# Carry scan over chunk ends: seven steps of one product each in place of four steps of up to three

## The reference

```python
# _ln: layer norm over the features
s = sigmoid(silu(x @ s_w1.T + s_b1) @ s_w2.T + s_b2)
u = (x @ B_w.T + B_b) * s                      # [b, t, 128]
def step(h, u_t):
    h = h @ A.T + u_t                          # A is 128 x 128
    return (h, h)
_, hs = scan(step, 0, u over t)
y = hs @ C_w.T + C_b + x @ D_w.T + D_b
attn = y * sigmoid(x @ g_w.T + g_b)            # x = x + ln(attn(ln(x)))
out_shared = sq_relu(xf @ Ws1) @ Ws2           # ffn, x = x + ln(ffn(ln(x)))
```

## Time and profile before

| what | value |
|---|---|
| median of 3 runs | 879.07 us (879.03 to 879.16) |
| the profiled execution, device time | 878.09 us |
| its span | 876.3 us |
| granted TensorE clock, mean over the span | 0.996 |
| DMA, mean | 84 GB/s |
| chain that ended last | ACT zn and DVE adds of the last rows, under 1% of the span each |

### The profile page before, as it was taken

One profiled execution on the slowest core, in us unless ns is written; L12 is line 12 of the kernel. 1 busy time (PEld: TensorE's weight loads), 2 busy tenths in 40 slices (PEclk: granted clock), 3 DMA queues, 4 the chain that ended last, 5 costly groups with the idle time before them and its releaser, 6 DMA issues. The chain is left out here.

```text
span 876.3 us, 12884 instructions
## 1 busy us (share of the span) xinstructions
PE 846.2 (97%) x4120; PEld 699.9 (80%) x4120; DVE 600.0 (68%) x1380; ACT 299.5 (34%) x530; POOL 374.5 (43%) x502
## 2 busy tenths in 40 slices
PE   5999999999999999999999999999999999999985
PEld 3778888888888888888888888888888888888874
DVE  5856775777757778577775777577775767844684
ACT  3431333323432334324342233333343323432333
POOL 0252336254344444253451633616334344435455
PEclk9999999999999999999999999999999999999999
DMA  9320303023220232221232230302323021122112
GB/s 306 127 97 0 97 27 146 21 97 96 95 99 24 73 96 97 98 72 44 77 117 77 96 96 16 144 35 97 96 83 111 3 94 49 49 96 97 49 48 97
DMA packets 17309, 73.23 MB, mean 84 GB/s; under 512 B 2643, under 2 KB 5075, under 8 KB 11094
## 3 DMA queue, kind: packets, MB, share of 16 engines
q1 hardware_dynamic: 17238, 72.38, 23.7%
HBM read 38.82 MB, written 33.55 MB: 83 GB/s over the span
## 5 line engine op out<-in xcount | busy, mean ns | idle before, releaser
L1624 POOL TENSOR_TENSOR xres<-work,xres 128x512 f32<-128x512 f32 x64 | 82.5, 1289 | 62.3 <-DVE work L1196 61.5
L433 PE MATMUL TM<-gw_hi,xT_hi 128*128 128x512 f32 x256 | 104.3, 407 | 0.0
L1588 POOL TENSOR_TENSOR rsz<-rsz,negh 128x1 f32<-128x1 f32 x64 | 39.4, 615 | 149.3 <-DVE rsz L1285 149.3
L433 PE MATMUL TM<-dw_hi,xT_hi 128*128 128x512 f32 x256 | 103.1, 403 | 0.0
L435 PE MATMUL TM<-dw_hi,xT_lo 128*128 128x512 f32 x256 | 100.5, 392 | 0.0
L435 PE MATMUL TM<-gw_hi,xT_lo 128*128 128x512 f32 x256 | 100.5, 392 | 0.0
L434 PE MATMUL TM<-gw_lo,xT_hi 128*128 128x512 f32 x256 | 100.0, 391 | 0.0
L434 PE MATMUL TM<-dw_lo,xT_hi 128*128 128x512 f32 x256 | 99.8, 390 | 0.0
L1588 POOL TENSOR_TENSOR rsv<-rsv,negh 128x1 f32<-128x1 f32 x64 | 35.8, 560 | 122.5 <-DVE rsv L1192 122.5
L1628 POOL TENSOR_TENSOR work<-work,xres 128x512 f32<-128x512 f32 x62 | 79.5, 1293 | 17.5 <-ACT work L908 17.5
L908 ACT ACTIVATE work<-TM,nmz,rsz 128x512 f32<-128x512 f32 x62 | 48.2, 778 | 69.3 <-POOL nmz L1598 69.1
(11 more groups left out here) (146 smaller groups left out, 2071.7 us busy)
## 6 DMA issues: line engine op xcount, KB each, us to landing
xin<-in_x SPq DMA_DIRECT2D x16, 1024.0 KB, 5.6
xres<-in_x SPq DMA_DIRECT2D x16, 1024.0 KB, 5.6
x_scratch<-xres SPq DMA_DIRECT2D x16, 1024.0 KB, 5.3
out<-work SPq DMA_DIRECT2D x30, 512.0 KB, 2.9
xres<-in_g_w_t SPq DMA_DIRECT2D x1, 1024.0 KB, 7.3
xres<-in_D_w_t SPq DMA_DIRECT2D x1, 1024.0 KB, 7.1
work<-in_Ws SPq DMA_DIRECT2D x2, 512.0 KB, 9.5
out<-work SPq DMA_DIRECT2D x4, 256.0 KB, 2.0
```

Source lines behind the costliest of these rows:

```text
L433: eng.matmul(ps, lhs[0], rhs[0], start=first, stop=False)
L1588: return eng.tensor_tensor(dst, src, negh[:, 0:n], ALU.pow)
L1624: eng.tensor_tensor(xres[:, j, :], work[:, j, :], xres[:, j, :], ALU.add).then_inc(S["x1_ok"], 1)
```

## The change

Steps 1 to 4 become steps 1 to 7 of one product each, with s = 1, 2, 4, ... 64: 7 products of 127, 126, 124, 120, 112, 96 and 64 columns in place of 10. The recurrence within the chunks is now steps 8 to 14. The powers A^24, A^96 and A^384 are no longer made, 21 products in the prologue for 24. The order of all engines is written anew, in the tails, the bodies and the prologue: among the rest the statistics and `h2` of DVE's tail stand elsewhere between the adds, `hs_low(3)` stands ahead of `ft_low(1)`, `SG(1)` ahead of `T(6)` and `T(7)`, and `s_gate(1)` of the prologue ahead of the high parts of f1 and f2. DMAs, their sizes and SP's order are the same. Line numbers below 460 stay, those of DVE's part shift by 12 (`scan_add`'s 1169, 1172 and 1175 are 1157, 1160 and 1163).

```diff
--- before.py
+++ after.py
@@ -76,7 +76,7 @@
-        POW = [1, 2, 3, 4, 5, 6, 7, 8, 16, 24, 32, 64, 96, 128, 256, 384, 512]
+        POW = [1, 2, 3, 4, 5, 6, 7, 8, 16, 32, 64, 128, 256, 512]
...
@@ -458,14 +458,11 @@
                     for j in range(L - 1):
                         m = eng.matmul(SC[:, 0:P], apt[:, idx[L - 1 - j], :], u[:, j, :],
                                        start=(j == 0), stop=(j == L - 2))
-                elif i <= 4:
-                    s = 4 ** (i - 1)
-                    reps = [r for r in (1, 2, 3) if r * s < P]
-                    for r in reps:
-                        m = eng.matmul(SC[:, r * s:P], apt[:, idx[L * s * r], :], carry[:, 1:1 + P - r * s],
-                                       start=(r == 1), stop=(r == reps[-1]))
+                elif i <= 7:
+                    s = 2 ** (i - 1)
+                    m = eng.matmul(SC[:, s:P], apt[:, idx[L * s], :], carry[:, 1:1 + P - s], start=True, stop=True)
                 else:
-                    j = i - 5
+                    j = i - 8
                     prev = carry[:, 0:P] if j == 0 else u[:, j - 1, :]
                     m = eng.matmul(SC[:, 0:P], apt[:, 0, :], prev, start=True, stop=True)
@@ -607,33 +604,31 @@
 
             def first_tail(b, rep):
                 a = (b, rep)
-                G(*a, 0, {1: 0})
-                scan_step(*a, 1)
-                G(*a, 1, {0: 2, 1: 3, 2: 4})
-                scan_step(*a, 5)
-                G(*a, 2, {1: 6, 2: 7})
-                scan_step(*a, 8)
-                scan_step(*a, 9)
-                G(*a, 3, {0: 10})
+                G(*a, 0, {0: 0, 2: 1})
+                scan_step(*a, 2)
+                G(*a, 1, {0: 3, 1: 4, 2: 5})
+                scan_step(*a, 6)
+                G(*a, 2, {0: 7, 1: 8, 2: 9})
+                scan_step(*a, 10)
                 scan_step(*a, 11)
+                G(*a, 3, {0: 12, 2: 13})
+                scan_step(*a, 14)
 
             def tail(b, rep):
                 a = (b, rep)
-                G(*a, 0)
-                scan_step(*a, 0)
-                W1f(*a, 1, 0, {0: 1, 2: 2})
-                scan_step(*a, 3)
-                W1f(*a, 1, 1, {2: 4})
-                scan_step(*a, 5)
-                G(*a, 1, {1: 6, 2: 7})
-                G(*a, 2, {1: 8})
-                scan_step(*a, 9)
+                G(*a, 0, {1: 0})
+                W1f(*a, 1, 0, {0: 1, 1: 2, 2: 3})
+                scan_step(*a, 4)
+                W1f(*a, 1, 1, {0: 5, 1: 6, 2: 7})
+                scan_step(*a, 8)
+                G(*a, 1, {0: 9})
+                G(*a, 2, {0: 10, 2: 11})
                 W2(*a, 4)
                 W2(*a, 5)
-                G(*a, 3, {1: 10})
+                G(*a, 3, {0: 12, 1: 13})
                 W2(*a, 6)
                 W2(*a, 7)
-                scan_step(*a, 11)
+                scan_step(*a, 14)
...
             def last_tail(b, rep):
                 a = (b, rep)
-                G(*a, 0, {2: 0})
-                scan_step(*a, 1)
-                W1f(*a, 1, 0, {0: 2})
-                W1f(*a, 1, 1, {0: 3, 1: 4})
+                G(*a, 0, {1: 0, 2: 1})
+                scan_step(*a, 2)
+                W1f(*a, 1, 0, {0: 3, 1: 4})
                 scan_step(*a, 5)
-                G(*a, 1, {0: 6})
-                scan_step(*a, 7)
-                G(*a, 2, {2: 8})
+                W1f(*a, 1, 1, {1: 6, 2: 7})
+                scan_step(*a, 8)
+                G(*a, 1, {0: 9, 2: 10})
+                G(*a, 2, {2: 11})
+                scan_step(*a, 12)
                 W2(*a, 4)
-                scan_step(*a, 9)
                 W2(*a, 5)
-                scan_step(*a, 10)
-                G(*a, 3)
+                G(*a, 3, {0: 13})
+                scan_step(*a, 14)
                 W2(*a, 6)
                 W2(*a, 7)
-                scan_step(*a, 11)
 
...
                 W2(*a, 3)
 
-            assert len(POWERS) == 24
+            assert len(POWERS) == 21
...
@@ -842,7 +833,7 @@
             def hs(b, rep, j):
 
                 if j < L - 1:
-                    eng.wait_ge(S["scan_ok"], body_at("scan_ok", b, 5 + j))
+                    eng.wait_ge(S["scan_ok"], body_at("scan_ok", b, 8 + j))
                 if j >= 2:
                     eng.wait_ge(S["y_done"], body_at("y_done", b, j - 2))
                 src = u[:, j, :] if j < L - 1 else carry[:, 1:P + 1]
...
@@ -1289,62 +1277,68 @@
                 scan_add(*a, 0)
                 ln1_stats(b + 1, 0)
                 scan_add(*a, 1)
+                scan_add(*a, 2)
                 ln1_stats(b + 1, 1)
-                scan_add(*a, 2)
-                ln1_stats(b + 1, 2)
                 scan_add(*a, 3)
                 scan_add(*a, 4)
-                ln1_stats(b + 1, 3)
+                ln1_stats(b + 1, 2)
                 scan_add(*a, 5)
                 scan_add(*a, 6)
-                ln1_norm(b + 1, 0)
                 scan_add(*a, 7)
+                ln1_stats(b + 1, 3)
                 scan_add(*a, 8)
                 scan_add(*a, 9)
-                ln1_norm(b + 1, 1)
-                ln1_norm(b + 1, 2)
-                hs_low(*a, 0)
-                hs_low(*a, 1)
-                ln1_stats(b + 1, 4)
                 scan_add(*a, 10)
                 scan_add(*a, 11)
+                scan_add(*a, 12)
+                ln1_norm(b + 1, 0)
+                hs_low(*a, 0)
+                scan_add(*a, 13)
+                ln1_stats(b + 1, 4)
+                ln1_norm(b + 1, 1)
                 ln1_stats(b + 1, 5)
+                scan_add(*a, 14)
                 ln1_stats(b + 1, 6)
                 ln1_stats(b + 1, 7)
+                ln1_norm(b + 1, 2)
+                hs_low(*a, 1)
                 ln1_norm(b + 1, 3)
 
             def tail(b, rep):
                 a = (b, rep)
                 scan_add(*a, 0)
+                ln1_stats(b + 1, 0)
                 scan_add(*a, 1)
                 scan_add(*a, 2)
-                ln1_stats(b + 1, 0)
                 scan_add(*a, 3)
-                h2(*a, 1, 0)
                 scan_add(*a, 4)
-                ln1_stats(b + 1, 1)
                 scan_add(*a, 5)
-                ln1_stats(b + 1, 2)
                 scan_add(*a, 6)
                 scan_add(*a, 7)
+                scan_add(*a, 8)
+                ln1_stats(b + 1, 1)
+                ln1_stats(b + 1, 2)
+                scan_add(*a, 9)
+                h2(*a, 1, 0)
+                scan_add(*a, 10)
+                h2(*a, 1, 1)
                 ln1_stats(b + 1, 3)
-                h2(*a, 1, 1)
-                scan_add(*a, 8)
+                scan_add(*a, 11)
                 ln1_stats(b + 1, 4)
-                scan_add(*a, 9)
                 z_stats(*a, 4)
+                scan_add(*a, 12)
                 z_stats(*a, 5)
-                scan_add(*a, 10)
                 ln1_stats(b + 1, 5)
+                ln1_norm(b + 1, 0)
+                scan_add(*a, 13)
+                z_stats(*a, 6)
+                ln1_norm(b + 1, 1)
                 hs_low(*a, 0)
                 hs_low(*a, 1)
-                ln1_norm(b + 1, 0)
-                z_stats(*a, 6)
-                ln1_norm(b + 1, 1)
+                ln1_norm(b + 1, 2)
                 z_stats(*a, 7)
                 ln1_stats(b + 1, 6)
-                ln1_norm(b + 1, 2)
-                scan_add(*a, 11)
+                scan_add(*a, 14)
                 ln1_norm(b + 1, 3)
                 ln1_stats(b + 1, 7)
 
```

267 lines of the change are left out of this document (132 added, 135 removed).

## The result

The changed kernel takes **890.81 us** (median of 4 runs, 886.03 to 892.37) against 879.12 for the kernel before, measured beside it (879.03 to 880.76). The ratio is 1.0119, 95% interval 1.0099 to 1.0139: slower by 11.7 us, where the forecast was 872.1 us and 0.93 on faster. Even the slowest end of my range, 876.2, is far off. The profiled execution has a span of 888.7 us, 12.4 more than the 876.3 of before.

What follows compares the result with a forecast made beforehand. PE, busy 97% of the span, was taken to set the time. Terms -5.0, -1.3, -1.2, -2.7, +2.1, +1.3, -0.4 sum to -7.2 us: 879.07 to 871.9, stated as 872.1 for missed waits; range 869.8 to 876.2.

Steps and rivals of the forecast that it cites:

- The first add of a loop turn: Loop turns' scan start: the 3.9 us lost around step 1's wait becomes 2.6 us at step 2, -1.3 us.
- The products: Scan on PE: seven single-product steps replace three of three products and one single, saving 0.63 us a batch, -5.0 us.
- The round trip: Scan steps: product, add and release take 0.77 us against 0.92 between steps, so PE does not stall.
- the round trip doesn't fit: Scan steps: add and release take over 0.92 us and each of seven steps pays; 888 us at 1.2 us, chance 0.02.
- Step 7 and hs_lo: Tail's step 7 and Y(3)'s C product: both waits go, 0.2 and 0.45 us a turn, -1.2 and -2.7 us.
- Waits in the tail: Loop tail behind add 8: W2 products wait for DVE work pushed back, 0.35 us a turn, +2.1 us.
- rivals 1 and 2: Only the products count, 875.9 us, chance 0.2; the tail turns to a chain on DVE, 875.8 us, chance 0.07.
- The first tail: First tail, run once: statistics between adds cause three waits of 0.35 us and 0.1 each, +1.3 us.
- Prologue and end: Prologue: u comes earlier, -0.4 us, from -1.5 to +1.0; end: a few tenths each way, counted at nothing.

Runs made afterwards that it cites:

- e8: The changed kernel with four one-element memsets more in VectorE's program ahead of its first load: 872.12 us.
- e3: The changed kernel with the prologue's orders of powers 5 to 9 and first transposes, and of their copies, as in the kernel before: 884.39 us.
- e10: The changed kernel with eight memsets more placed behind the loop, ahead of the last tail, where they shift nothing of the loop: 889.64 us.
- e2: The changed kernel with the loop tail's first statistics of x moved from behind add 0 to behind add 8: 884.18 us.
- e4: The kernel before with three one-element memsets more in VectorE's program ahead of its first load: 889.26 us.
- e11: The changed kernel with two memsets more in VectorE's program ahead of its first load: 885.09 us.

## Why the prediction was wrong, point by point

**The step that failed** is "The first add of a loop turn". I had the loop edge in a row (2.45 us ahead of add 0), called it "the loop's own edge on DVE", and carried it over as a fixed price of one gap in front of add 0. "Step 2 waits some 0.25 to 0.5 us" rests on that. It is not a price of the jump (the free kernels have the same jump at 0.3 us) but of instructions that have to be brought in again, and it comes back at the next edge between stretches. In the kernel before, the second edge lay behind add 2, under a wait of 1.76 us. The change put the loop three instructions later in the program (head 315, not 312), put statistics at the edge, and took the cover away as well. The term was -1.3 us, 3.9 before less 2.6 after. Measured, the waits are 10.2 us, and the clock comes on top: turns 2 to 6 take 16.5 us more in sum than in e8, the same loop four places further.

**The clock** was in no term. Behind 7 of the 15 waits of 1.7 to 2.2 us in the loop (the changed kernel, e3, e10) PE ran at half clock for 3.41 us, at a cost of some 1.4 to 1.7 us each (turns of 106.2 to 106.6 against 104.5 to 104.9). At the wait of 2.3 us in the last batch it was 13 of 17. Behind the waits of up to 0.7, 1.1 and 1.6 us in the loop (e2, e4, e11, five turns each) there was no drop. That the runs of the changed kernel spread over 6 us would fit a number of drops that differs from run to run, but only one of them was profiled. Which wait is followed by a drop and which isn't was not settled.

**The products**, -5.0: confirmed as far as the rows go. In all of e8's tails the next matmul starts 0.14 us behind a single step and the one after it 0.31 to 0.32 later, whether the step has 127 columns or 64; and in the kernel before a step of 112, 96 and 80 columns takes 0.59 us to the next matmul against 0.58 for 124, 120 and 116, a row that the prediction used without showing it. Steps are 0.92 us apart and one record pair long:

```profile
154.18 0.38 PE L463 MATMUL SC<-carry,apt 128*128 128x127 f32 x2
...
155.09 0.38 PE L463 MATMUL SC<-carry,apt 128*128 128x126 f32 x2
...
156.02 0.38 PE L463 MATMUL SC<-carry,apt 128*128 128x124 f32 x2
```

In batch 7 of e8 no wait of the scan hides anything: step 0 to the first D product is 25.57 us, before 25.36. Step 0 now stands one k group of 0.69 us earlier, so 0.48 us are saved, where I had 0.63. With the 0.45 of hs_lo in the body ahead of it this makes the 0.9 that e8 gains up to the mark of batch 7.

**The round trip** of 0.77 us held in each of e8's loop tails, with 0.92 between steps and no wait. My one rival on the slower side (the round trip doesn't fit, 0.02) gave a time near the measured one, 888 us, by a mechanism that did not happen; the right one, what the new place of the loop could cost, I did not have.

**Step 7 and hs_lo**, -1.2 and -2.7: both waits went. **Waits in the tail**, +2.1: none came; the order had more room than I worked out. With the last at nothing, my terms for turn 1 are -0.63 - 0.2 - 0.45 = -1.28; measured between the marks, -1.12 in the changed kernel and -1.24 in e8. So rivals 1 and 2 did not happen either.

**The first tail**, +1.3: three waits came, as said. The steps that waited stand 1.20, 1.19 and 1.17 us behind the step before instead of 0.92, and the step behind each of them 1.02 or 1.03, which makes +1.1. The first two of the three:

```profile
61.15 0.38 PE L463 MATMUL SC<-carry,apt 128*128 128x124 f32 x2
...
62.35 0.48 PE L463 MATMUL SC<-carry,apt 128*128 128x120 f32 x2
...
63.37 0.37 PE L463 MATMUL SC<-carry,apt 128*128 128x112 f32 x2
...
64.56 0.46 PE L463 MATMUL SC<-carry,apt 128*128 128x96 f32 x2
```

**Prologue and end**, -0.4 and nothing: wrong in sign. e8 has the clock pattern of before (full at 16.9, half from 23.8 to 27.2 us; before 16.6, 23.5 to 26.9), and its step 0 comes at 52.90 us against 52.76 although it stands 0.69 us earlier in the order: +0.8, inside my bound of +1.0. The end costs +1.1 (e8 against before, last product to the end), which I had put at nothing as "a few tenths each way"; whether the flag or the last add sets it was not separated.

Set against each other for e8, whose loop is at a free place: start to batch 0's mark +1.3, turn 1 -1.2, turns 2 to 6 -9.7 (104.4 to 102.5 each, of which about 0.6 each is the edge that went), batch 7 -0.9, end +1.0: -9.6 us of span, 866.7 against 876.3. The profile of the changed kernel is 22.0 us longer than e8's: 16.5 of it in turns 2 to 6, 3.4 ahead of batch 0's mark, where full speed came late, and 2.0 behind that of batch 7.

That e8's median, 872.12 us, is the forecast of 872.1 to the digit is luck. My terms made -7.2 of what is -9.6 between the two profiles: the waits of the tail (+2.1) never came, the wait at the loop's edge went wholly (by my own working -3.9 and not -1.3), and prologue and end cost 1.8 us where I had -0.4. The profiled execution of e8 is 3.6 us faster than its median besides. What held is the mechanism in the loop: single steps at 0.92 us, no wait between them, hs_lo and step 7 gone.
